# An attention kernel's hand-written order: first maxima moved behind the second scores, three small tasks spread over three steps

## What is computed

```
state = q
for _ in range(STEPS):
    sim = jnp.einsum('bqhd,bkhd->bqhk', state, k)
    att = jax.nn.softmax(BETA * sim, axis=-1)
    state = jnp.einsum('bqhk,bkhd->bqhd', att, v)
o = state.reshape(B, S, H) @ Wo + bo
return residual + o
```

## Time and profile before

| | us |
|---|---|
| median of 3 runs | 1473.08 (1471.55 to 1474.25) |
| profiled execution, from the first to the last instruction | 1467.2 |
| of it the first attention with its prologue, about | 0 to 507 |
| busy over the span: PE, DVE, ACT, POOL | 1305.1, 1130.4, 969.6, 751.3 |
| mean granted clock of PE | 0.954 of 2.4 GHz |

### The profile page before, as it was taken

One profiled execution on the slowest core, in us unless ns is written; L12 is line 12 of the kernel. 1 busy time (PEld: TensorE's weight loads), 2 busy tenths in 40 slices (PEclk: granted clock), 3 DMA queues, 4 the chain that ended last, 5 costly groups with the idle time before them and its releaser, 6 DMA issues. The chain is left out here.

```text
span 1467.2 us, 34194 instructions
## 1 busy us (share of the span) xinstructions
PE 1305.1 (89%) x12121; PEld 987.2 (67%) x12121; DVE 1130.4 (77%) x3054; ACT 969.6 (66%) x1498; POOL 751.3 (51%) x961
## 2 busy tenths in 40 slices
PE   2899999999998689899927999999999998699997
PEld 1566666666654367899915777777777776588886
DVE  5578889889875667899956888888888776567776
ACT  1688888888886447777723777777777777343441
POOL 4775665787852363799866455455444220101112
PEclk9899999999998779999958999999999999799999
DMA  6000000111111021122121111111111110134353
GB/s 234 18 23 20 22 20 20 28 32 28 31 36 30 8 80 32 56 73 73 58 87 51 49 47 48 46 48 47 49 46 38 39 42 18 26 92 116 80 129 82
DMA packets 84430, 77.20 MB, mean 53 GB/s; under 512 B 18224, under 2 KB 72240, under 8 KB 83888
## 3 DMA queue, kind: packets, MB, share of 16 engines
q1 hardware_dynamic: 80176, 66.73, 17.1%
q0 software_dynamic: 4096, 8.40, 2.0%
HBM read 36.26 MB, written 13.63 MB: 34 GB/s over the span
## 5 line engine op out<-in xcount | busy, mean ns | idle before, releaser
L541 ACT ACTIVATE a_p<-a_ps_s 128x1024 f32<-128x1024 f32 x256 | 258.3, 1031 | 25.1 <-PE a_ps_s L400 22.2
L651 DVE TENSOR_REDUCE a_qt<-a_ps_d 128x2 fp32r<-128x512 f32 x256 | 174.6, 687 | 48.9 <-PE a_ps_d L411 44.9
L1298 DVE TENSOR_REDUCE a_qt<-a_ps_d 128x2 fp32r<-128x512 f32 x256 | 173.3, 688 | 44.9 <-PE a_ps_d L1086 39.9
L822 POOL TENSOR_TENSOR a_rn<-a_ss,a_half 128x16 f32<-128x16 f32 x56 | 162.6, 2920 | 1.3
L1203 ACT ACTIVATE a_pg<-a_ps_s 128x1024 f32<-128x1024 f32 x128 | 125.8, 1024 | 26.8 <-PE a_ps_s L1075 25.4
L418 PE MATMUL a_ps_o<-a_p,a_v 128*32 128x256 f32 x2048 | 129.5, 393 | 3.7 <-ACT a_p L541 3.7
L1086 PE MATMUL a_ps_d<-a_kpad,a_qs 128*128 128x512 f32 x256 | 126.0, 495 | 5.8 <-DVE a_qt L1298 2.7
L411 PE MATMUL a_ps_d<-a_kpad,a_qs 128*128 128x512 f32 x256 | 126.8, 496 | 4.3 <-DVE a_qt L651 2.4
L2300 ACT ACTIVATE f_s<-f_ps_g 128x512 f32<-128x512 f32 x72 | 43.0, 598 | 99.9 <-PE f_ps_g L2246 99.7
L1494 POOL DMA_INDIRECT a_picked<-ys,rows x64 | 67.6, 1056 | 61.8 <-PE a_ps_d L1086 50.8
L418 PEld LDWEIGHTS a_ps_o<-a_p,a_v 128*32 128x32 f32 x2048 | 61.2, 112 | 52.9 <-issue 22.3
(11 more groups left out here) (355 smaller groups left out, 3823.9 us busy)
## 6 DMA issues: line engine op xcount, KB each, us to landing
a_kpad<-a_kc SPq DMA_DIRECT2D x512, 32.0 KB
f_gb<-spread SPq DMA_DIRECT2D x64, 256.0 KB, 5.7
a_kpad<-a_kq SPq DMA_DIRECT2D x256, 32.0 KB, 1.8
f_xin<-xs SPq DMA_DIRECT2D x39, 128.0 KB, 2.1
ys<-f_yout SPq DMA_DIRECT2D x39, 128.0 KB, 2.1
w<-in_w SPq DMA_DIRECT2D x2, 2304.0 KB, 11.4
out_x<-X SPq DMA_DIRECT2D x8, 256.0 KB, 6.8
xs<-f_zero SPq DMA_DIRECT2D x15, 128.0 KB
```

The lines of the kernel that those rows point to most:

```text
L541: nc.scalar.activation(probs[:, u % 2, 2 * c:2 * c + 2, :, :].rearrange("p a b c -> p (a b c)"), ps_s[:, 2 * c:2 * c + 2, :].rearrange("p ...
L651: nc.vector.tensor_reduce(qt2[:, (k - PEAK) % 4, 2 * part:2 * part + 2, SHIFT], bank(k, f"m{part}")[:, :].rearrange("p (a b) -> p a b", b= ...
L822: nc.gpsimd.tensor_tensor(rn[:, part * c:(part + 1) * c], ss[:, part * c:(part + 1) * c], half[:, 0:c], ALU.pow).then_inc(rn_ready, 1)
L1298: nc.vector.tensor_reduce(qt[:, b % 2, GLOBAL, n:n + 2, SHIFT], bank(k, f"m{part}")[:, :].rearrange("p (j s) -> p j s", s=S), AX.X, ALU.ma ...
```

## The change

It moves code in PE's and ACT's loops and adapts the counts:

- `maxima(st, 0)` goes from before the attends to behind the second scores, and the second scores go ahead of `maxima(st, 1)` (and of "qp"): first scores, attends, second scores, then the first, second and third maximum in a row.
- the transposes of yT, xT and zT all stand between first scores and attends, in steps r = 2, 3 and 0; before they were in steps 2, 2 and 3. "qp" now waits for the xT of the same step, the router's product for the zT of the same step.
- ACT's copies of xT and zT move between the two first exponentials, where yT's was.

```
-    A_ORDER = ("yT", "xT", "T", "zT", "KQ")
+    A_ORDER = ("yT", "xT", "zT", "T", "KQ")
...
-                    "yT": r == 2 and batch(b - 2), "xT": r == 2 and batch(b + 3),
-                    "zT": r == 3 and 0 <= b - 3 < ROUTED}[task]
+                    "yT": r == 2 and batch(b - 2), "xT": r == 3 and batch(b + 3),
+                    "zT": r == 0 and 0 <= b - 4 < ROUTED}[task]
...
                     scores(k, q_of(k))
-                if unit(k - PEAK):
-                    u = k - PEAK
-                    pe.wait_ge(kpad_loaded[u % PAD_RING], 64 * (u // PAD_RING + 1))
-                    pe.wait_ge(a_done, a_count(k - 1, "T"))
-                maxima(st, 0)
                 if a_live(k, "yT"):
...
                     transposes(ps_a, lambda t: out2[:, b % 2, t, :], a_full)
+                if a_live(k, "xT"):
+                    pe.wait_ge(z1_ready, b + 4)
+                    wait_a(st, "xT")
+                    transposes(ps_a, lambda t: z1[:, t, :], a_full)
+                if a_live(k, "zT"):
+                    pe.wait_ge(z_new, b - 3)
+                    wait_a(st, "zT")
+                    transposes(ps_a, lambda t: Z[:, ((b - 4) * TPB + t) * D:((b - 4) * TPB + t + 1) * D], a_full)
                 if unit(k - 1) or unit(k - LAST_USE):
...
                     last.then_inc(o_full, 1)
-                if a_live(k, "xT"):
-                    pe.wait_ge(z1_ready, b + 4)
-                    wait_a(st, "xT")
-                    transposes(ps_a, lambda t: z1[:, t, :], a_full)
-                if projects:
-                    pe.wait_ge(a_done, a_count(k - 1, "xT"))
-                    project(st, 0, "qp")
-                maxima(st, 1)
                 if unit(k - SECOND):
...
                     scores(k - SECOND, qs2[:, (k - 1) % 2, S:2 * S])
+                if unit(k - PEAK):
+                    u = k - PEAK
+                    pe.wait_ge(kpad_loaded[u % PAD_RING], 64 * (u // PAD_RING + 1))
+                    pe.wait_ge(a_done, a_count(k - 1, "T"))
+                maxima(st, 0)
+                if projects:
+                    pe.wait_ge(a_done, a_count(k, "xT"))
+                    project(st, 0, "qp")
+                maxima(st, 1)
                 maxima(st, 2)
```

More of the change, by code:

```diff
@@ L498, in _ @@
                     pe.wait_ge(a["later"], 16 * a["laters"])
-                    pe.wait_ge(a_done, a_count(k - 1, "zT"))
+                    pe.wait_ge(a_done, a_count(k, "zT"))
                     wait_d(st, "lg")
@@ L512, in _ @@
                     project(st, 1, "kp")
[L513 to L516, removed]
                 if projects:
@@ L559, in _ @@
                     copy_a(st, "yT", yT[:, :])
+                if a_live(k, "xT"):
+                    act.wait_ge(a_full, a_count(k, "xT"))
+                    nc.scalar.activation(xT[:, :], ps_a[:, 0:S], ACT.Identity, scale=a["ln_w"][:, 0:1],
+                                         bias=a["ln_b"][:, 0:1]).then_inc(a_done, 1)
+                if a_live(k, "zT"):
+                    copy_a(st, "zT", zT[:, :])
                 if unit(k):
@@ L577, in _ @@
                     nc.scalar.copy(ot[:, live], ps_o[:, live]).then_inc(o_copied, 1)
[L578 to L581, removed]
                 if unit(k - SECOND):
@@ L588, in _ @@
                     exps(st, 3, k - SECOND, p2)
-                if a_live(k, "zT"):
-                    copy_a(st, "zT", zT[:, :])
                 if unit(k + NG):
@@ L693, in _ @@
                     if batch(b + 2):
-                        dve.wait_ge(a_full, a_count(k - NG, "xT"))
+                        dve.wait_ge(a_full, a_count(k - 3, "xT"))
                     zz = rows_of(Z, st, 3)
```

## The result

The changed kernel takes 1537.64 us (1533.39 to 1539.66, 4 runs) against 1472.32 beside it: 1.0443 times, interval 1.0424 to 1.0463. The forecast was 1539. The profiled execution spans 1534.5 us; 1533 was the sum.

What follows compares the result with a forecast made beforehand. No engine has much to spare; a step is a round trip between them. Batches of 32.05 us and smaller terms give +66 on a 1467.2 span, 1533, plus 5.9: 1539 us; forecast 1525 to 1555 (0.68), range 1504 to 1585.

Steps and rivals of the forecast that it cites:

- S: Start of a step's second scores on TensorE in the first attention; the prediction counts its times from there.
- The wait for the bank: Third maximum waits for the first reduction: S+1.72 instead of S+0.43, cast of turned queries S+2.70 instead of S+1.48; costs 1.22.
- The saving ahead of S: First exponential to second scores: 2.10 us instead of 2.59, since two maxima no longer stand there; saves 0.49 a step.
- the plain loop: Step of the first attention without side work or moved copies: 7.01 us instead of 6.28, 0.73 lost.
- VectorE's side work and the results behind it: Work between first and second reduction delays later reductions and results: steps of 7.95 at r = 1, 7.6 at r = 0.
- The copies between the exponentials: Casts of yT, xT, zT on ScalarE lie on the loop: 0.25 each for yT and zT, 0.5 for xT.
- The sum by stretches: Steps 5 to 51 +56, following 11 steps +5, last steps +3, router work +2, prologue and later stages 0: +66 us.
- Faster: Rival: reductions keep up and only the saving is left, 29 us, 1444; third maximum below S+0.5; chance 0.04.
- The clock: Rival: TensorE's idle pieces in the new step bring half-clock spells, one a batch adding 42 to 70: 1581 to 1609; chance 0.15.
- The upper bound of 1550: All VectorE and TensorE waits of r = 0, 1, 3 on the path, plus all of today's extra 13 us: +77.

Runs made afterwards that it cites:

- The halved reductions: VectorE's maxima over the first 128 of 256 keys: in the changed kernel 1499.6 us (1.0191), in the kernel before, as control, 1469.98 us (0.9993).
- the side work moved away: Changed kernel with VectorE's sum of squares (r = 0) and statistics and addition (r = 1) ahead of the first reduction: 1511.59 us, 1.0296.
- the experiment with the turned queries: Changed kernel with the turned queries directly behind the second scores, ahead of the first three maxima: 1573.12 us, 1.0687.
- The kernel with the first maximum ahead: Kernel before with only the transposes and copies of yT, xT, zT moved, plus first maximum ahead of first scores at r = 1 and 2: 1468.76 us, 0.9981.
- the kernel with ScalarE's copies moved: Changed kernel with ScalarE's copies of xT and zT behind the second of the two first exponentials instead of between them: 1533.34 us, 1.0412.

## Why the prediction was right

From S to S the four steps of the batch shown took 7.87, 7.48, 8.90 and 7.46 us (r = 1, 2, 3, 0), 31.71 in all; forecast were 7.95, 7.6, 8.9 and 7.6, 32.05.

- **The wait for the bank.** The forecast was S+1.72 for the third maximum and S+2.70 for the cast; the trace has S+1.72 and S+2.69 (358.98). The halved reductions move it by their own amount, and move nothing in the kernel before.
- **The saving ahead of S.** The forecast was 2.10 from first exponential to S; at r = 1 the trace has 2.00 (354.29 to 356.29, where it was 2.59), so the plain loop is 6.91 and not 7.01, and the step r = 0 with the side work moved away takes just that, 6.90. In the timeline above the second scores at r = 1 and r = 3 wait for the second of the two first exponentials (356.29, 371.64, 388.00: `<-ACT a_p`), so there the saving is taken; in the other two steps they follow the attends without a wait, and the attends set them. The saving was there, and it was smaller than the wait.
- **VectorE's side work and the results behind it.** The forecast was 1.5 us a batch above the loop of 7.01 for r = 0 and r = 1; they stand 0.45 and 0.86 above it, and moving the work away takes 1.2 off. Had I stopped at the plain loop, the forecast would have been 1504, and the experiment with the turned queries shows why that would be wrong: there the loop through the cast is short again, and the chain of reductions alone holds every step.
- **The copies between the exponentials** were mis-sized: forecast 1.0 us a batch for the three; of xT's and zT's 0.75 only 0.34 was on the path. The term ignored that the attends, held by the moved transposes, end nearly as late. Behind the step r = 3 zT's transposes wait for the cast of k and q, which reads the one bank of `ps_a` (378.33, 0.33 `<-ACT a_kq`); the forecast had them hidden. The step still came out at 8.9, since the attends gave the S that the forecast had from the exponentials: the right number for another reason.
- **The sum by stretches.** Steps 5 to 51 took 446.30 - 70.75 = 375.6 (forecast 376.5 and 2 of router work), the following 11 steps 86.5 (87.3). From the 63rd result copy to the last it takes 35.0, where the kernel before took 29.5 (its last copy is at 503.92): +5.4 instead of +3. The stages behind took 3.4 us more (966.7 instead of 963.3), which was not forecast. The change need not have done that: their code is the same in all twelve kernels profiled here, and they take from 959.6 to 966.7 us. So the batches came out 3 us shorter than the sum had them, the last steps 2 longer and the stages behind 3 longer. That the total is right to 2 us is luck; that each stretch is right to 3 is not.
- **The rivals.** Faster: excluded by the third maximum's start. The clock: the stretch stayed at 0.99, but see below. TensorE was busy 86%, not 80%: I had counted up to 2 us of 8 as idle, and it was idle for 66.8 us in 58 steps, 1.15 each. The forecast's own sum would have given 82% (382.7 of 464). The upper bound of 1550 takes 13 us as today's extra in the last 11 steps; the rows give 9 (82.3 against 11 x 6.7).

The Trainium skill, TensorEngine Tiling (Array Packing), Key Properties, says that a change of tiling mode drains TensorE. The trace agrees as far as starts go: behind a maximum the next one starts 0.23 later (two of 0.50 in 0.73) and a full-width transpose 0.34 later (358.01 to 358.35), but the column-tiled attends 0.43 later (340.30 to 340.73 in the kernel before). So a switch costs 0.2 us at most here; that a drain is the cause no run shows. The change has two such switches fewer in a plain step and one fewer where transposes stand ahead of the attends. The kernel with the first maximum ahead saves one without the wait for the bank, but only at r = 1, since at r = 2 yT's full-width transposes stay between the first scores and the attends. The step r = 1 gains 0.12 us by it and r = 2 nothing, some 2 us of the whole kernel. It is not what decides.

## What to carry to other kernels

Before moving work of a two-bank rotation, write down when each bank is read: matmuls that are cheap to issue in a row are not cheap if the reader takes 0.69 us for each and something urgent stands behind the third. A producer's work placed early, under another long group, gives its reader time for free; the same work in a row puts the reader on the path, with everything else that the reader does in between. And when one wait is removed, look for the next chain of nearly the same length before counting the gain: here taking the cast's wait away made the kernel slower, since what took its place put every reduction 0.4 us later.

## What was unexpected

The clock rival was half right, in places that I had not named. In the two steps of the changed kernel where the router's placement stands between maxima (10.1 and 10.4 us between result copies at steps 33 and 49), TensorE waited for reductions and then ran at 1.2 GHz for a while. Busy times by engine around step 33 (windows, columns as in rows 1), TensorE with 0.76 us of waits in the first and at half clock in the second:

```profile
292.00:294.70 2.70, 1.94 (x15) 1.66 (x15) 2.54 (x8) 1.59 (x3) 0.00 (x0) 1.00 0.00 0
294.70:298.10 3.40, 3.35 (x19) 2.25 (x18) 2.98 (x17) 0.66 (x2) 1.15 (x2) 0.51 0.12 28
```

The long step 61 (9.7 us) is another matter: there TensorE and VectorE stood still, much as around 462 in the kernel before. The third maximum waited 4.11 us (526.35) for a reduction that itself came after 5.56 idle us of VectorE, whose end the profile puts down to `remote`, and then the clock fell (0.58 from 526.30 to 530.00). What it was no run shows.

The kernel with the turned queries first meets the lower clock again and again. Its first 47 steps of the stretch, one step r = 1 at full clock, and a piece of the step shown above:

```profile
71.21:479.07 407.86, 344.82 (x3318) 212.97 (x3322) 268.70 (x876) 276.29 (x388) 225.36 (x208) 0.94 0.08 19
...
348.18:356.44 8.26, 6.32 (x70) 3.66 (x66) 5.45 (x21) 5.63 (x8) 2.72 (x5) 1.00 0.08 18
...
421.90:424.80 2.90, 2.86 (x26) 1.48 (x28) 2.64 (x17) 2.04 (x4) 2.01 (x3) 0.50 0.21 51
```

There TensorE waits 0.55 and 0.81 us before the third and fourth maximum, and the piece behind them is granted 0.50, the lower level; over these steps the mean is 0.94, where the changed kernel's stretch has 0.99. The slow piece has a pair of transposes at 0.64 instead of 0.38 and the attends at 2.60 instead of 1.93, and the step takes 9.27 us where the same step at full clock, with the same order and the same waits, takes 8.26. One such spell comes in nearly every batch and costs 1.0 to 1.3 us, some 14 us in 47 steps.

What decides whether a given step meets it no run here shows: in the kernel with ScalarE's copies moved a step r = 0 fell to 0.80 behind waits of 0.55 and 0.34 that its neighbours had as well. The section "A second HAM failure mode: psum-queue depth-cycling" of the Trainium skill's page TensorE: Matmul & The Clock Gate describes such a case, a kernel that cycles through PSUM banks and whose clock swings between its two levels with short idle times of TensorE between matmul groups, and the trace of that experiment agrees; in the changed kernel itself it stayed rare.

In the kernel with the side work ahead the half clock in the two placement steps near 33 and 49 is absent: they take 8.5 us from S to S instead of 9.9 and 10.1, together 1.7 us more off than the moved work explains. In the profiled executions its stretch is 17.0 us shorter, with those 1.7 in it, the last steps 1.2, and the stages behind the first attention 6.3 (960.4 us instead of 966.7), whose code did not change. So most of its gain above the 17 us is not the side work's.
